# A gated cross-attention and expert layer on one core: similarity rows transposed in column groups and spread from three row groups, contexts in quarters, a new schedule

## The reference

```python
# cosine similarity over the channels, of every context column with its left neighbour, itself and its right one
sim = stack([cos(emb, emb_left), cos(emb, emb), cos(emb, emb_right)])     # 3 rows of 1024 per batch
att = repeat(sim, C, axis=1)                                             # one row for each of 3*128 unfolded rows
out = einsum('bit,oi->bot', unfold(layernorm(x), 3) * att, w_flat)        # a convolution with 3 taps
x = x + tanh(g_xattn) * out
# then experts: top 2 of 8, rank 16, on layernorm(x)
logits = flat @ router_w.T + router_b;  gates = top 2 of softmax, made to sum to 1
h = einsum('nd,erd->ner', flat, A);  out = einsum('ner,eor->no', h * w, Bm) * 0.5
x = x + tanh(g_ffn) * out
```

## Time and profile before

| | before |
|---|---|
| median of three runs | 226.66 us |
| the profiled execution | 228.04 us |
| its span in the trace | 226.2 us |
| TensorE busy | 210.0 us (93% of the span) |
| VectorE busy | 173.7 us (77%) |
| ScalarE busy | 114.4 us (51%) |
| GpSimd busy | 61.3 us (27%) |
| mean granted TensorE clock | 0.962 of full |

### The profile page before, as it was taken

The page is one execution under the profiler, slowest core; times in us unless marked ns, Lnnn a source line. Parts: engine busy times, 40 slices in busy tenths (PEclk is TensorE's granted clock), DMA queues, the critical chain, the costliest instruction groups (busy, mean ns, idle before and its releaser), DMA issues.

```text
span 226.2 us, 3735 instructions
## 1 busy us (share of the span) xinstructions
PE 210.0 (93%) x1006; PEld 121.1 (54%) x1006; DVE 173.7 (77%) x481; ACT 114.4 (51%) x208; POOL 61.3 (27%) x150
## 2 busy tenths in 40 slices
PE   5566699999999999999999999999999999999883
PEld 5126123646575545466665545475756566657461
DVE  2444749588988799679979798779988787877574
ACT  4466971555485756434476556453575353421220
POOL 2010663112224532212224552203131313202030
PEclk9796569999999999999999999999999999999999
DMA  6969700625131313609050502222232202020107
GB/s 177 385 218 360 298 6 0 194 88 211 71 127 59 119 72 117 254 4 353 18 185 1 185 0 93 93 85 101 64 122 93 96 0 94 0 96 28 64 0 280
DMA packets 8766, 27.21 MB, mean 120 GB/s; under 512 B 1616, under 2 KB 2128, under 8 KB 8752
## 3 DMA queue, kind: packets, MB, share of 16 engines
q1 hardware_dynamic: 8752, 27.05, 33.3%
HBM read 18.65 MB, written 8.39 MB: 120 GB/s over the span
## 4 chain that ended last, share of the span: by engine, by line
PE 77%; DVE 6%; DMA 5%; issue 4%; SPq 3%; ACT 2%; POOL 1%; DVEq 0%; ACTq 0%; POOLq 0%
PE bank L906 34%; PE bank L930 12%; PE bank L895 9%; PE bank L915 6%; PE bank L862 5%; DMA xt<-x 5%; PE bank L949 3%; PE bank L953 3%; PE bank L950 3%; DVE pt L642 2%; DVE x L658 1%; DVE pr L650 1%; PE bank L939 1%; SPq L246 1%; DVE x L722 1%
## 5 line engine op out<-in xcount | busy, mean ns | idle before, releaser
L906 PE MATMUL bank<-pt,wT 128*128 128x512 f32 x192 | 100.8, 608 | 0.0
L642 DVE TENSOR_TENSOR pt<-xn,bank 128x512 f32<-128x512 f32 x96 | 65.2, 681 | 14.7 <-PE bank L895 8.8
L472 ACT ACTIVATE xT<-bank 128x512 f32<-128x512 f32 x32 | 19.1, 595 | 47.8 <-PE bank L915 47.8
L906 PEld LDWEIGHTS bank<-pt,wT 128*128 128x128 f32 x192 | 32.0, 193 | 20.5 <-issue 9.6
L895 PE MATMUL bank<-rows,sel 96*128 96x512 bf16 (+1 forms) x96 | 37.8, 396 | 1.9 <-ACT rows L438 1.2
L930 PEld LDWEIGHTS bank<-aT,xT 128*128 128x128 f32 x256 | 33.0, 190 | 5.5 <-issue 4.1
L930 PE MATMUL bank<-aT,xT 128*128 128x136 f32 x256 | 34.8, 279 | 0.0
L658 DVE TENSOR_TENSOR x<-bank,xt 128x512 f32<-128x512 f32 x32 | 22.1, 690 | 8.5 <-PE bank L906 8.2
L895 PEld LDWEIGHTS bank<-rows,sel 96*128 96x128 bf16 x96 | 9.3, 98 | 28.4 <-issue 19.6
L722 DVE TENSOR_TENSOR x<-bank,x 128x512 f32<-128x512 f32 x32 | 21.1, 665 | 1.8 <-PE bank L953 1.8
L664 DVE BATCH_NORM_STATS2 bn<-x 128x6 f32<-128x512 f32 x32 | 21.8, 681 | 0.0
(11 more groups left out here) (90 smaller groups left out, 246.6 us busy)
## 6 DMA issues: line engine op xcount, KB each, us to landing
et<-ctx SPq DMA_DIRECT2D x16, 512.0 KB, 6.1
xt<-x SPq DMA_DIRECT2D x16, 512.0 KB, 3.4
out<-x SPq DMA_DIRECT2D x15, 512.0 KB, 2.6
aT_in<-expert_aT SPq DMA_DIRECT2D x1, 544.0 KB, 9.4
bm_in<-expert_b SPq DMA_DIRECT2D x1, 512.0 KB, 10.3
out<-x SPq DMA_DIRECT2D x2, 256.0 KB, 2.0
sel<-select SPq DMA_DIRECT2D x1, 288.0 KB, 11.0
wT_in<-conv_wT SPq DMA_DIRECT2D x1, 192.0 KB, 10.4
```

Of the source, the lines that this page charges most:

```text
L472: nc.scalar.activation(xT[:, j % 2, 4 * h:4 * h + 4, :].rearrange("p c n -> p (c n)"), xT_ps[:, :], ACT.Copy).then_inc(xT_out, 1)
L642: nc.vector.tensor_tensor(pt[:, i, :], xn[:, j % 2, h * HALF + k:(h + 1) * HALF + k], sim_ps[i % 2][:, :], ALU.mult).then_inc(mod_done, 1)
L906: nc.tensor.matmul(conv_ps[h][:, :], wT[:, k * P:(k + 1) * P], pt[:, i, :], start=(k == 0), stop=(k == TAPS - 1)).then_inc(tap_done, 1)
```

## The change

- **Groups.** The 16 batches go in groups of 1, 3, 3, 3, 3, 3 (`GROUPS`). The loops are written out in full, and tables give the batch and step at which each context is squared, folded and summed.
- **Contexts in quarters.** A context is loaded by another access pattern: partition p gets, from each block of 32 channels, 257 neighbouring values of quarter-rows (pieces of 1,028 bytes instead of 4 KB), so that no shifted copy crosses a partition. Squares and products lie in one tile `qp` of four blocks. A sum over channels is then four blocks of matmuls with 128 columns, four abreast in column groups. For contexts 7 to 15, GpSimd first adds blocks 2 and 3 onto 0 and 1 (`fold`), and two blocks are left.
- **Products.** GpSimd makes those of contexts 1, 3 and 4, VectorE the other 13.
- **Norms.** GpSimd's `inverse_norms` takes the power -0.5 of 32 columns in one operation, in place of VectorE's guess and Newton steps. `next_norms` has six matmuls instead of two, and shifts the dot products too. The split into bf16 parts has four operations instead of five.
- **Rows.** The similarity parts of a tap are transposed to 32 partitions of their own: 24 transposes of 32 columns a group, in three column groups. A spread is then three matmuls of 32 rows each, from three row groups, into three banks, issued together once a half.
- **Experts.** The gates come from one sigmoid on ScalarE and six operations of GpSimd (`weigh_experts`), in the last batch of VectorE. VectorE reads the logits out of PSUM and makes `hwT_lo`.
- **Banks.** Three banks hold the spread rows. `xT_ps` is shared with the transposed contexts, the shifted norms and the transposed rows; `out_ps` with `hwT_ps`; `h_ps` with the context sums. Waits are added where a bank has several users.
- **The start.** It is made for one context only, with idle matmuls (`keep_warm`) between its steps; the means of `aT_in` are summed by GpSimd and need one matmul. SyncE waits for GpSimd's memsets before it loads `sel`.

The diff, cut to its core (the lines removed are those of the functions above):

```diff
+WARM_UP = 6
...
+GROUPS = ((0,), (1, 2, 3), (4, 5, 6), (7, 8, 9), (10, 11, 12), (13, 14, 15))
...
+FOLDED = 7
...
+SQUARES, FOLDS = {(0, 3): 4, (1, 1): 5, (1, 4): 6}, {}
+SUMS = {(0, 1): 2, (0, 2): 3, (1, 0): 4, (1, 5): 5, (2, 0): 6}
+for e in range(7, 16):
+    SQUARES[e - 6, 5] = FOLDS[e - 5, 0] = SUMS[e - 5, 5] = e
+TURNS, NEIGHBOURS, ROWS = {(0, 3): 1}, {(0, 4): 1}, {(1, 0): 1}
+for q, (f, *_) in list(enumerate(GROUPS))[2:]:
+    TURNS[f - 2, 3 if q == 2 else 0], NEIGHBOURS[f - 2, 5 if q == 2 else 3], ROWS[f - 1, 0] = q, q, q
...
+ON_POOL = (1, 3, 4)
...
+        et = sb("et", [P, G, 4, QUARTER + 1])
...
+        qp = sb("qp", [P, G, 2, 4, QUARTER])
...
+        sim_ps = st.enter_context(nc.psum_tensor("sim_ps", [P, TAPS, HALF], F32))
...
+        rows_ps = xT_ps[:, :].bitcast(BF16)
...
+        hwT_ps = out_ps[:, 0:P]
...
+        h_ps, sum_ps = hidden_ps[:, 0:ER + E], hidden_ps[:, 256:256 + P]
...
+            def load_e(e):
+                if e >= G:
+                    sp.wait_ge(sq_done, e - G + 1)
+                    wait_for_product(sp, e - G)
+                def piece(p0, p1, c0, c1, times):
+                    src = bass.AP(tensor=ctx.tensor, offset=e * P * T + c0 * 32 * T + p0 * QUARTER,
+                                  ap=[[QUARTER, p1 - p0], [32 * T, c1 - c0], [1, times]])
+                    sp.dma_start(et[p0:p1, e % G, c0:c1, 0:times], src).then_inc(e_in[e % G], 16)
+                if e < B - 1:
+                    piece(0, P, 0, 4, QUARTER + 1)
+                else:
+                    piece(0, P, 0, 3, QUARTER + 1)
+                    piece(0, P - 1, 3, 4, QUARTER + 1)
...
+            load_e(0)
+            sp.dma_start(ident, identity).then_inc(ident_in, 16)
+            load_x(0)
+            load_e(1)
+            sp.dma_start(gates_in[:, 0:1], g_xattn.rearrange("(a n) -> a n", a=1).to_broadcast([P, 1])).then_inc(gates_in_done, 16)
+            sp.dma_start(gates_in[:, 1:2], g_ffn.rearrange("(a n) -> a n", a=1).to_broadcast([P, 1])).then_inc(gates_in_done, 16)
+            sp.dma_start(identb[:, :], identity_bf).then_inc(identb_in, 16)
+            sp.wait_ge(setup, SETUP)
+            load_sel(0, sel0_in)
+            sp.dma_start(wT_in[:, :], conv_wT).then_inc(conv_in, 16)
+            load_e(2)
...
+            def product(e):
+                if e >= G:
+                    pool.wait_ge(summed, e - G + 1)
+                pool.wait_ge(e_in[e % G], loads_up_to(e))
+                nc.gpsimd.tensor_tensor(qp[:, e % G, 1, :, :], et[:, e % G, :, 0:QUARTER], et[:, e % G, :, 1:QUARTER + 1],
+                                        ALU.mult).then_inc(pr_pool_done, 1)
...
+            def fold(e):
+                pool.wait_ge(sq_done, e + 1)
+                wait_for_product(pool, e)
+                nc.gpsimd.tensor_tensor(qp[:, e % G, :, 0:2, :], qp[:, e % G, :, 0:2, :], qp[:, e % G, :, 2:4, :],
+                                        ALU.add).then_inc(folded, 1)
...
+            def inverse_norms(q):
+                pool.wait_ge(nmax_done, q + 1)
+                if q >= 1:
+                    pool.wait_ge(rnext_done, q)
+                    pool.wait_ge(sim_done, 3 * q)
+                nc.gpsimd.tensor_tensor(rinv[:, :], nmax[:, :], minus_half[:, :], ALU.pow).then_inc(rinv_done, 1)
...
+            def weigh_experts(n):
+                i = n % 2
+                if n == 0:
+                    pool.wait_ge(ffn_in, 16 * 2)
+                pool.wait_ge(topi_done, n + 1)
+                nc.gpsimd.tensor_copy(topf[:, i, :], topi[:, i, 0:2]).then_inc(topf_done, 1)
+                pool.wait_ge(w2_done, n + 1)
+                nc.gpsimd.tensor_tensor(g2[:, i:i + 1], w2[:, i:i + 1], rs2[:, i:i + 1], ALU.mult).then_inc(g2_done, 1)
+                pool.wait_ge(g2_done, n + 1)
+                nc.gpsimd.tensor_tensor(g1[:, i:i + 1], rs2[:, i:i + 1], g2[:, i:i + 1], ALU.subtract).then_inc(g1_done, 1)
+                pool.wait_ge(topf_done, n + 1)
+                nc.gpsimd.tensor_scalar(gb[:, i, :], ids[:, :], topf[:, i, 1:2], g2[:, i:i + 1], ALU.is_equal,
+                                        ALU.mult).then_inc(picked, 1)
+                pool.wait_ge(g1_done, n + 1)
+                nc.gpsimd.tensor_scalar(ga[:, i, :], ids[:, :], topf[:, i, 0:1], g1[:, i:i + 1], ALU.is_equal,
+                                        ALU.mult).then_inc(picked, 1)
...
+            def columns_copy(q):
+                dve.wait_ge(ctxT_done, q + 1)
+                if q >= 1:
+                    dve.wait_ge(rinv_done, q)
+                members = len(GROUPS[q])
+                of_batches = [tile.rearrange("p (z m b) -> p z m b", z=2, b=G)[:, :, :, 0:members]
+                              for tile in (nmax[:, :], columns[:, 0, :], columns[:, 1, :])]
+                squared, product_sums = columns_ps[:, 0, :, :, 0:members], columns_ps[:, 1, :, :, 0:members]
+                nc.vector.tensor_scalar(of_batches[0], squared, COS_EPS * COS_EPS, None, ALU.max).then_inc(nmax_done, 1)
+                nc.vector.tensor_copy(of_batches[1], squared).then_inc(columns_out, 1)
...
+            def similarities(q):
+                members = slice(0, 3)
+                flat = sim[:, :, :, :].rearrange("p c b f -> p c (b f)")
+                part = [simp[:, :, i:PARTS * NINE:PARTS] for i in range(PARTS)]
+                dve.wait_ge(partial, 2 * (q + 1))
+                if q >= 1:
+                    dve.wait_ge(rowsT_done, q)
+                nc.vector.tensor_tensor(sim[:, :, :, 1], chunked(nr[:, :])[:, :, members], chunked(rinv[:, :])[:, :, members],
                                         ALU.mult).then_inc(sim_done, 1)
+                yield
+                dve.wait_ge(rnext_done, q + 1)
+                nc.vector.tensor_tensor(sim[:, :, :, 0], chunked(dr[:, :])[:, :, members], chunked(rnext_ps)[:, :, members],
...
+            late = iter(())
+            for n in range(B):
+                picks = pick_experts(n - 1) if n >= 1 else iter(())
+                for i in range(STEPS):
+                    if n >= 1 and (n, i) in NEIGHBOURS:
+                        take(late, 2)
+                        late = similarities(NEIGHBOURS[n, i])
+                    if (n, i) in ROWS:
+                        take(late, 7)
+                        rows_low(ROWS[n, i])
+                    if i == 0 and n >= 1:
+                        residual(n - 1, 1)
+                    if n >= 1 and (n, i) in TURNS:
+                        columns_copy(TURNS[n, i])
+                        late = partials(TURNS[n, i])
+                    if n == 1 and i == 0:
...
+                    if n >= 1 and i == 0 or n == 0 and i == 2:
+                        modulate(STEPS * n + 3)
+                        take(late)
+                        modulate(STEPS * n + 4)
+                        take(late)
...
+                    if i == 3 and n >= 1:
+                        residual(n, 0)
+                        take(late)
+                    if i == 3 and 1 <= n < B - 1:
+                        modulate(STEPS * (n + 1))
+                        take(late)
+                        modulate(STEPS * (n + 1) + 1)
+                        take(late)
+                        modulate(STEPS * (n + 1) + 2)
+                    if i == 4:
+                        if n >= 2:
+                            finish(n - 2, 1)
+                        take(late)
+                        if n >= 1:
+                            token_stats(n, 0)
+                        take(late)
+                    if i == 5 and n >= 1:
...
+            def sum_context(e, hidden=0):
+                if e < FOLDED:
+                    pe.wait_ge(sq_done, e + 1)
+                    wait_for_product(pe, e)
+                else:
+                    pe.wait_ge(folded, e - FOLDED + 1)
+                if e >= 1:
+                    pe.wait_ge(sums_out, e)
+                if e == GROUPS[2][0]:
+                    pe.wait_ge(aT_done, 1)
+                if hidden:
+                    pe.wait_ge(h_out, hidden)
...
+                pieces = 4 if e < FOLDED else 2
+                for c in range(pieces):
+                    for r in range(4):
+                        z, what = r // 2, r % 2
+                        last = nc.tensor.matmul(sum_ps[32 * r:32 * r + 32, :], onehot[:, :],
+                                                qp[:, e % G, what, c, z * P:(z + 1) * P], start=(c == 0), stop=(c == pieces - 1))
...
+            def next_norms(q, tokens):
+                pe.wait_ge(rinv_done, q + 1)
+                pe.wait_ge(partial, 2 * q + 1)
+                if tokens:
...
+                z1, z2, more = slice(0, 4 * G), slice(4 * G, 8 * G), 3 * G
+                nc.tensor.matmul(rnext_ps, to_next, rinv[:, :], start=True, stop=False)
+                nc.tensor.matmul(rnext_ps[:, z1], to_next_chunk, rinv[:, z2], start=False, stop=False)
+                nc.tensor.matmul(rnext_ps[:, 4 * G:4 * G + more], to_next_chunk, rinv[:, G:G + more], start=False, stop=True)
```

(37 more changed lines are left out.)

1192 lines of the change are left out of this document (517 added, 675 removed).

## The result

The changed kernel takes 278.07 us (median, 275.3 to 282.5) where the kernel before took 226.95 in the same comparison: a ratio of 1.2205, 95% interval 1.2104 to 1.2307. It is slower by 22%. Ratios here compare the faster of two states that a kernel's executions fall into, and medians take in both, so 278.07 has one slower execution in it (282.5) that 1.2205 leaves out. The forecast was 220.5 us with a range up to 233, so the sign and the range were both wrong. The profiled execution took 278.2 us, with a span of 276.4.

What follows compares the result with a forecast made beforehand. TensorE was taken to bound the middle, with VectorE second at 83%. Start 35.0, middle 173.5 and end 11.5 summed to 220.0 us against a span of 226.2, hence a median of 220.5; range 210 to 233.

Steps and rivals of the forecast that it cites:

- The power: GpSimd's inverse norms on 32 columns: 1.5 us taken, between bounds of 0.55 and 17.6.
- the first rival: The power is slow and VectorE waits for it in order; gain gone at 2.5 us, 235.5 at 4; chance 0.15.
- The rival's slope: Each microsecond of power above 1.5 costs the start two and each of four groups one: 6 us.
- The second rival: VectorE falls behind, blocked beside GpSimd's folds in two groups and at `hidden_rest`: 7.8 us, so 228; chance 0.17.
- Spreads: TensorE, middle: sets of three abreast at 0.35 us, 29 x 0.35 = 10.2 against 18.7 before; gain 8.5.
- where I gave 4.0: TensorE stalls in the middle: 1.0 us for each of three groups and 1.0 for everything else.
- the 169.5 of the sum: TensorE's middle before stalls: 172.9 - 8.5 - 1.5 + 5.3 + 1.3 = 169.5 us.
- Start and end: First tap at 18.2 us instead of 27.3, batch 1's at 35.0 instead of 40.5; end 11.5 instead of 12.7.
- the row transposes: TensorE, once a group: 24 row transposes, between 0.44 + 0.19 and 1.5 us, taken 0.8.
- the folded sum: TensorE, context sums: 0.75 us folded instead of 1.18, bounds 0.59 and 1.18; gain 1.5 in all.
- the turn batch: Batch where a group is turned: VectorE 13.0 us against TensorE's 12.65; TensorE stalls 0.5 to 1.0, taken as 1.0.

Runs made afterwards that it cites:

- run 4: Kernel before, with GpSimd's power of 32 columns in place of VectorE's ten Newton operations: 243.03 us, ratio 1.0622.
- run 1: Changed kernel with GpSimd's power replaced by a multiplication of the same 128x32 tiles: 243.87 us, ratio 1.0676.
- run 6: Changed kernel with the power on the columns in use alone (8 of 32 for the first group, 24 for the others): 268.51 us, ratio 1.1676.
- run 7: Changed kernel with the power replaced by a multiplication and no context folded: 234.5 us, ratio 1.0268.
- 8: Changed kernel, power kept, with no context folded: 270.4 us, ratio 1.1847.
- run 5: Kernel before, with a multiplication of 32 columns on GpSimd in place of VectorE's ten Newton operations: 227.18 us, ratio 0.9991.
- 11: Changed kernel, power replaced by a multiplication, no folds, expert matrix scaled, rounded and its low part taken in batch 0: 232.57 us, ratio 1.0246.
- 15: Changed kernel with power on 8 or 24 columns, no folds, low part in batch 0, shifts, row transposes and VectorE's partial products later: 256.65 us, no ratio.

## Why the prediction was wrong, step by step

**The power, the step that failed.** The sum had 1.5 us for an instruction that takes 5.44. The bounds in the text were 0.55 and 17.6, and I took the value near the free end because small operations on GpSimd are mostly fixed cost, "as a product of 1,023 columns at 1.89 shows (under 2 ns a column)". That row is of a multiplication. The only rows of a power were of one column, where 0.55 us beside 0.19 for an addition of the same size (in run 4's trace) says that a power is another kind of work: three times the price on one column. At 0.157 us a column it is some 85 times dearer by the column than the product, and a multiplication of the same 32 columns takes 0.25 us. Between ends that far apart the value should have been the middle, or the chance of the first rival far above 0.15.

**The rival's slope was nearly right.** It gave 6 us for each microsecond of a power, 23.6 for 5.44 instead of 1.5. Run 1 took 5.19 us from each power and 34.7 from the time, 6.7 for each microsecond; run 6 took 10.1 us from six powers and 12.0 from the time. By the first, 26 of the 34.7 us are what the mis-sized price did to the sum (34.7 x 3.94 / 5.19, an estimate), and the rest a power of 1.5 us would have cost as well. In the traces, 18.6 us lie in the start (batch 1's first tap 51.7 against 33.1) and 18.3 in the middle (212.2 against 193.9). The start has more than its two powers of 5.19, and the first tap, 10.2 us later than in run 1, shows why. VectorE and GpSimd in the changed kernel, then VectorE in run 1:

```profile
19.16 1.57 DVE L632 CAST simp<-sim 128x72 bf16<-128x72 f32 x1
20.76 1.25 DVE L635 TENSOR_TENSOR rest<-sim,simp 128x72 f32<-128x72 f32 x1
...
16.89 3.74 POOL L353 TENSOR_TENSOR qp<-et 128x1024 f32<-128x1024 f32 x2
...
13.27 0.58 DVE L632 CAST simp<-sim 128x72 bf16<-128x72 f32 x1
```

Up to `dr` it is 5.0 us late. The shifts add 0.9, at a granted clock of 0.50 where run 1 has 1.00. The four splits, which now meet GpSimd's products and sums of `aT_in`, take 4.3 us instead of 1.5 and add 2.8. From the row transposes to the tap, again at 0.50, come another 1.5.

**Folds against VectorE.** The second rival had the mechanism and the place, 7.8 us; the runs give 10 to 13 (7 and 8), and not in two groups alone: the early batches have them too. The Trainium skill, SBUF — State Buffer, Who interferes with whom, describes that hold, for VectorE's instructions with two inputs in SBUF and for its copies and casts in a two-port mode, and leaves out instructions with at most one SBUF input outside these modes. The rows agree: `dr`, a similarity and a product with both inputs in SBUF were held up beside a fold or the low part (2.32, 2.23 and 2.77 us), while modulations, which read `sim_ps` in PSUM, took 0.68 us beside a fold as without it, and the statistics 0.69.

**Spreads.** A set is 0.52 us, not 0.35: the change of layout costs 0.09 ahead and 0.10 behind, as at the context sums, and the three cost 0.33 together, not 0.22. Over 29 sets that is 4.9 us. The Trainium skill, TensorEngine Tiling (Array Packing), Key Properties, has a drain at each change of tiling mode. The trace agrees with it: 0.19 of the 0.52 us are the changes, where my 0.35 left 0.13 for them, and three spreads abreast cost another 0.11 over the 0.22 of one.

**Batches 1 to 3.** In run 7 (its table row of the middle) TensorE is idle 8.7 us, where I gave 4.0, and busy 180.5:

```profile
31.82:221.00 189.18, 180.46 (x1238) 108.05 (x1239) 147.15 (x334) 92.32 (x174) 57.87 (x179) 0.99 0.26 96
```

Less 3.9 for the unfolded sums, that is 176.6 against the 169.5 of the sum: 4.9 of the 7.1 are the spreads, and the rest fits the clock of 0.99 (it is 0.91 in the 20 us from 44 to 64 and full elsewhere). From batch 4 on, the lengths follow the forecast (turn batches 13.8, ordinary ones 11.6 with an unfolded sum). Of the idle time, 6.4 us lie in batches 1 to 3, with waits for `hwT_lo`, `sums`, `simp` and a residual. I take the reason to be the work that the new start no longer does and that these batches now have; that was argued from the schedule and not tried. Batch 1's first tap comes at 31.8, 3.2 us ahead of the forecast, but 2.5 of these are the two powers, which run 7 does not have.

**What was right.** Start and end without the power (17.7, 33.1, 11.7 against 18.2, 35.0, 11.5, of which the powers were to take 1.5 and 3.0 in the start), the row transposes (0.55, taken 0.8), the folded sum (0.57 + 0.1, taken 0.75), the turn batch.

**The account.** Between the forecast of 220.5 and 278.1 us lie 57.6. Step by step, in ratios of 226.95 us: 34.7 from the changed kernel to one without the power, 9.3 from there to one without the folds either, and 12.5 from that one to the forecast (the ratio of 1.2205 gives 277.0 us, 1.1 under the median). Of the 12.5, 3.9 are the unfolded sums and 4.9 the spreads. With the power as good as free and without the folds, the kernel is still 2.7% slower than before (2.0 to 3.4). And run 5 shows that one exchange could not have paid: in the kernel before, Newton's ten operations were hidden behind TensorE, and with them gone the time is the same (0.9991, 0.9968 to 1.0013).

**Still open.** Why the three spreads abreast take 0.33 and not 0.22 was not tried. Nor was what batches 1 and 2 wait for beside the low part taken apart.

## What to carry to other kernels

Before an operation moves to another engine, run the kernel with it left out: here that one run says that there is nothing to win. Price an instruction by rows of its own operation; if there is only one row, at one size, its fixed and per-column parts are unknown, and both bounds stay alive. A long instruction on GpSimd also delays every small one behind it, so look for who waits for those. And while GpSimd adds or multiplies 1024 columns, VectorE's operations with two inputs in SBUF and its casts there stand still, so place it beside VectorE's work on PSUM, or leave it out.

## What the runs showed of the hardware

- A power of float32 on GpSimd: 0.55 us on one column, 1.67 on 8, 4.18 on 24, 5.44 on 32 (128 partitions). A multiplication of 32 columns: 0.25.
- An addition of 1024 columns on GpSimd takes 2.36 us where the product of as many takes 1.89. The subtraction that writes fp32r takes 2.36 to 2.37 too (runs 11 and 15, and the kernel before), and 3.42 where it begins together with a product on VectorE: it is held up as well.
- VectorE beside GpSimd's additions, products and subtraction: two-input operations of 24 to 32 columns in SBUF 2.2 to 2.3 us instead of 0.17 to 0.2, a product 2.77 instead of 1.2. Not slowed: operations with an operand in PSUM (modulations 0.68), and statistics, which read one SBUF input (0.69).
- VectorE beside GpSimd's power: an operation on 8 columns in SBUF took 0.22 us, three times of three; beside a product its like took 1.89 (run 4).
- Three matmuls abreast in row groups of 32: 0.33 us, with 0.09 ahead and 0.10 behind, 0.52 in all; three of 96 rows one after another 0.65, with nothing ahead.
- TensorE after a stretch of 4 us with 0.16 us of work: 10 us at a granted clock of 0.51.
